# A four-layer hybrid kernel on one core: the last mamba chunk's gating and normalisation moved, one drive given to ScalarE, the mixtures' last lists moved ahead

## The reference

```python
x = x + mamba(_layernorm(x))       # 256 channels, 16 states each, a scan over 2048 tokens
x = x + ffn(_layernorm(x))         # mixture of 8 experts
x = x + attention(_layernorm(x))   # linear attention, head size 64
x = x + ffn(_layernorm(x))         # the same mixture again

def _layernorm(x, eps=1e-05):
    return (x - mean(x)) / sqrt(var(x) + eps)
# mamba: x_m, z = split(x @ W_in); x_m = silu(conv(x_m) + conv_b); dt = softplus(...)
#   state = exp(dt * A) * state + dt * B * x_m ;  y = sum_s(state * C) + x_m * D
#   out = (y * silu(z)) @ W_out
# ffn: scores = (tanh(x @ gate_w.T) + 1) / 2; each expert takes its 512 best tokens (top_k);
#   layernorm, two layers with gelu, times the score, added at the tokens' rows (at[idx].add)
```

## Time and profile before

| what | us |
|---|---|
| time, median of 3 runs | 832.78 (832.06 to 836.05) |
| the profiled execution | 831.78 |
| its span | 830.0 |

### The profile page before, as it was taken

The page is one execution under the profiler, slowest core; times in us unless marked ns, Lnnn a source line. Parts: engine busy times, 40 slices in busy tenths (PEclk is TensorE's granted clock), DMA queues, the critical chain, the costliest instruction groups (busy, mean ns, idle before and its releaser), DMA issues. The chain is left out here.

```text
span 830.0 us, 11428 instructions
## 1 busy us (share of the span) xinstructions
PE 621.2 (75%) x3747; PEld 465.3 (56%) x3747; DVE 569.7 (69%) x1030; ACT 504.8 (61%) x1020; POOL 605.9 (73%) x427
## 2 busy tenths in 40 slices
PE   6767999799996999967778824999462871489842
PEld 4334766577674777746667713766342760367531
DVE  6357998989989898999998687423115669832210
ACT  2257999879899779997889366423112359222300
POOL 6019899999999999998899571778861026378875
PEclk8987999989998999989899955899885995589967
DMA  5044765745546475565453065523334004053332
GB/s 155 0 132 134 220 213 179 231 155 203 222 166 199 161 237 185 160 216 182 183 189 132 1 197 147 156 40 40 40 28 111 1 1 102 21 156 43 39 36 25
DMA packets 71131, 104.52 MB, mean 126 GB/s; under 512 B 15545, under 2 KB 49122, under 8 KB 71074
## 3 DMA queue, kind: packets, MB, share of 16 engines
q1 hardware_dynamic: 59122, 93.58, 35.3%
q0 software_dynamic: 11264, 8.66, 7.8%
q10 hardware_dynamic: 688, 1.57, 0.7%
HBM read 90.12 MB, written 13.63 MB: 125 GB/s over the span
## 5 line engine op out<-in xcount | busy, mean ns | idle before, releaser
L412 POOL TENSOR_TENSOR product<-state,c_all 128x1024 f32<-128x1024 f32 x128 | 301.9, 2401 | 19.8 <-DVE state L730 16.2
L934 PE MATMUL m_psum<-ident,product 128*128 128x128 f32 x1024 | 137.8, 280 | 10.0 <-POOL product L412 5.0
L934 PEld LDWEIGHTS m_psum<-ident,product 128*128 128x128 f32 x1024 | 118.5, 145 | 31.5 <-issue 14.3
L730 DVE TENSOR_TENSOR_SCAN state<-decay,carry,m_psum 128x1024 f32<-128x1024 f32 x56 | 129.5, 2336 | 5.3 <-issue 2.7
L545 ACT ACTIVATE decay<-dt,decay_rate 128x1024 f32<-128x1024 f32 x112 | 126.8, 1143 | 10.2 <-DVE state L730 8.3
L730 DVE TENSOR_TENSOR_SCAN state<-decay,m_psum 128x1024 f32<-128x1024 f32 x56 | 125.9, 2276 | 8.8 <-PE m_psum L958 3.4
L523 ACT ACTIVATE drive_T<-dtu_T,b_T 128x128 f32<-128x128 f32 x416 | 130.0, 394 | 0.9 <-PE m_psum L958 0.7
L1453 ACT ACTIVATE f_f_T<-f_psum,f_b_T 128x512 f32<-128x512 f32 x64 | 44.0, 688 | 136.2 <-PE f_psum L1712 136.2
L1394 POOL DMA_INDIRECT f_got<-f_table,f_tokens x64 | 65.4, 1021 | 56.8 <-DVE f_tokens L1563 41.0
L836 PE MATMUL m_psum<-xn_T,w_tap 128*128 128x512 f32 (+2 forms) x128 | 71.6, 673 | 21.6 <-DVE dt L677 16.0
L958 PE MATMUL m_psum<-ident,drive_T 128*128 128x128 f32 x544 | 74.0, 280 | 9.9 <-DVE state L730 9.6
(11 more groups left out here) (266 smaller groups left out, 1086.9 us busy)
## 6 DMA issues: line engine op xcount, KB each, us to landing
c_all<-cb_dram SPq DMA_DIRECT2D x128, 512.0 KB, 4.1
b_all<-cb_dram SPq DMA_DIRECT2D x16, 512.0 KB, 4.9
f_table<-f_rows SPq DMA_DIRECT2D x2, 2176.0 KB, 12.2
X<-in_L_attn_a_x SPq DMA_DIRECT2D x4, 512.0 KB, 7.3
f_w_raw<-in_L_ffn_fc2s SPq DMA_DIRECT2D x1, 2048.0 KB, 17.6
between<-f_f SPq DMA_DIRECT2D x1, 2048.0 KB, 9.2
X<-between SPq DMA_DIRECT2D x4, 512.0 KB, 6.1
out<-f_f SPq DMA_DIRECT2D x1, 2048.0 KB, 9.3
```

Source lines behind the costliest of these rows:

```text
L412: pool.tensor_tensor(product[:, n % RING, :], state[:, n % RING, :], c_all[:, n % RING, :], ALU.mult).then_inc(product_ready, 1)
L730: dve.tensor_tensor_scan(state[:, n % RING, :], flat(pair(n)) if alone else decay[:, n % RING, :], lone_drive[:, made(n, "lone") % LONES, ...
L934: last = pe.matmul(psum[:, Y + i // BT, i % BT * P:(i % BT + 1) * P], product[:, n % RING, i * P:(i + 1) * P], ident[:], start=(s == 0 and ...
```

## The change

1. Epsilon goes into the bias of ScalarE's square root (a new tile `eps`, filled by POOL at the start). VectorE's separate add of epsilon goes, in all layer norms: four times in the mamba layer (L628), four in each front (L1069) and once more where a front normalises its result a second time (L1094), twice in attention (L1817).
2. In the last chunk, drive 6 changes from 'd' to 'a'.
3. In the last chunk, z's matmuls stand at TensorE's steps 15 to 18 (before 15, 18, 19, 22). Roots and Silus stand together at ScalarE's step 21 (before: roots at 15, Silus at 25). VectorE's two scale operations stand at step 22 (before 16 and 17). ScalarE normalises at steps 25 to 30 (before 20 to 27), and TensorE turns those tiles at 27, 28, 29 and 31 (before 25 to 28).
4. In the mixtures lists(3) stands earlier on TensorE, ahead of `turn_rows(0)`, and in mixture 1 ahead of six weight turns too; VectorE takes them ahead of `scale_rows(0, 0)`. The first weight turn stands at search step 6 instead of 5 (`LATE`).

```diff
-        MEASURE_AT, AGGREGATE_AT, ROOT_AT, SCALE_AT, NORMALISE_AT = FRONT + 1, FRONT + 9, FRONT + 15, FRONT + 16, FRONT + 20
+        MEASURE_AT, AGGREGATE_AT, SCALE_AT, NORMALISE_AT = FRONT + 1, FRONT + 9, FRONT + 22, FRONT + 25
+        LAST_SILU, BY_STEP = FRONT + 21, (0, 3, 6, 9, 12, 14, 16)
...
-        MAKERS = ('dddqqadpadaaadad', 'qdaaqaddaapppdaa')
+        MAKERS = ('dddqqadpadaaadad', 'qdaaqaddaapppdaa') * 3 + ('dddqqaapadaaadad', 'qdaaqaddaapppdaa')
...
-        F_AT = (25, 26, 27, 28)
+        F_AT, LAST_Z_AT = (27, 28, 29, 31), (15, 16, 17, 18)
...
-                if n == ROOT_AT:
+                if n == LAST_SILU:
                     act.preload_act_table(ACT.Sqrt)
                     for q in range(2):
                         front["root"](act, q)
-                    act.preload_act_table_set("natural_log_exp_and_others")
...
-                if n % PERIOD == SILU:
+                if (n == LAST_SILU) if g + 1 == CHUNKS else (n % PERIOD == SILU):
                     silu(g)
...
-                    if n == SCALE_AT + q:
+                    if n == SCALE_AT:
                         front["scale"](dve, q)
...
-        dve.wait_ge(aggregated, QT * (q + 1))
-        dve.tensor_scalar(rstd[:, part(q)], moments[:, part(q), 1], LN_EPS, None,
-                          ALU.add).then_inc(variance, 1)
 
     def root(act, q):
-        act.wait_ge(variance, q + 1)
-        act.activation(rstd[:, part(q)], rstd[:, part(q)],
-                       ACT.Sqrt).then_inc(std_done, 1)
+        act.wait_ge(aggregated, QT * (q + 1))
+        act.activation(rstd[:, part(q)], moments[:, part(q), 1], ACT.Sqrt,
+                       bias=eps[:]).then_inc(std_done, 1)
...
-    SCORES, LATE, MIDWAY = 4, 5, 6
+    SCORES, LATE, MIDWAY = 4, 6, 6
...
+        take_lists(3)
         scale_rows(0, 0)
-        take_lists(3)
...
-            for n in range(MIDWAY, 2 * E):
+            for n in range(MIDWAY, MIDWAY + 4):
+                turn_weights(n)
+        lists(3)
+        if first_use:
+            for n in range(MIDWAY + 4, 2 * E):
                 turn_weights(n)
...
         turn_rows(0)
-        lists(3)
```

More of the change, by code:

```diff
@@ L33, in layer_norm_constants, with mamba @@
     return at + 2 * tiles
-def mamba(nc, X, ident, w_tap, early, front, home, gate_w, x, W_in, conv_w, conv_b, A_log, D, W_x, W_dt, b_dt, W_out):
+def mamba(nc, X, ident, eps, w_tap, early, front, home, gate_w, x, W_in, conv_w, conv_b, A_log, D, W_x, W_dt, b_dt, W_out):
     BATCH, L, DM = x.shape
@@ L221, in beside @@
             out += [("turn", g, 1, t, (TURN_AT[1],)) for t in range(TB)]
-            out += [("z", g, i // TB, i % TB, (Z_AT[i],)) for i in range(KB * TB)]
+            out += [("z", g, i // TB, i % TB, ((Z_AT if g + 1 < CHUNKS else LAST_Z_AT)[i],)) for i in range(KB * TB)]
             out += [("back", g, 0, t, (BACK_AT[0],)) for t in range(TB)]
@@ L452, in std @@
             def std(first, end):
-                act.wait_ge(variance, end)
-                part = rstd[:, first * CT:end * CT]
-                act.activation(part, part, ACT.Sqrt).then_inc(std_done, 1)
+                act.wait_ge(dve_chain, 2 * CT * end + (1 if first else 0))
+                part = slice(first * CT, end * CT)
+                act.activation(rstd[:, part], moments[:, part, 1], ACT.Sqrt, bias=eps[:]).then_inc(std_done, 1)
             def take_turned(g):
@@ L592, in _ @@
                         front["root"](act, q)
-                    act.preload_act_table_set("natural_log_exp_and_others")
-                if n >= NORMALISE_AT and 2 * (n - NORMALISE_AT) < 2 * QUARTER:
+                if NORMALISE_AT <= n < NORMALISE_AT + len(BY_STEP) - 1:
                     if n == NORMALISE_AT:
                         act.wait_ge(summed, FRONT)
-                    front["normalise"](act, "a", 2 * (n - NORMALISE_AT), 2 * (n - NORMALISE_AT) + 2)
-                if n % PERIOD == SILU:
+                    front["normalise"](act, "a", *BY_STEP[n - NORMALISE_AT:n - NORMALISE_AT + 2])
+                if (n == LAST_SILU) if g + 1 == CHUNKS else (n % PERIOD == SILU):
                     silu(g)
@@ L606, in _ @@
                         drive_by_act(n + ahead, first, first + CT // 2)
+            for number, piece in enumerate(PIECES):
+                if piece[0] in ACT_LATER and piece[4] and piece[4][-1] + ACT_LATER[piece[0]] >= STEPS:
+                    take(piece, number)
             act.preload_act_table(ACT.Sqrt)
@@ L627, in token_stats @@
                                           lambda i: X[:, g * CT + i, :], CT)
-                dve.tensor_scalar(rstd[:, tiles], moments[:, tiles, 1], LN_EPS, None,
-                                  ALU.add).then_inc(variance, 1)
                 return at
@@ L1010, in _ @@
         def _(pool):
+            pool.memset(eps[:], LN_EPS)
             pool.memset(ident[:], 0.0).then_inc(zeroed, 1)
@@ L1024, in front_tiles, with front_of @@
             for what, shape in shapes.items()}
-def front_of(nc, tiles, name, X, home, banks, scores, gate_pad, makers, takers):
+def front_of(nc, tiles, name, X, home, eps, banks, scores, gate_pad, makers, takers):
     def sem(what):
@@ L1091, in variance_again @@
         dve.tensor_tensor(again[:], again[:], moments[:, :, 1],
-                          ALU.mult).then_inc(link, 1)
-        dve.wait_ge(link, 2)
-        dve.tensor_scalar(again[:], again[:], LN_EPS, None, ALU.add).then_inc(variance2, 1)
+                          ALU.mult).then_inc(variance2, 1)
     def root_again(act):
         act.wait_ge(variance2, 1)
-        act.activation(again[:], again[:], ACT.Sqrt).then_inc(std2_done, 1)
+        act.activation(again[:], again[:], ACT.Sqrt, bias=eps[:]).then_inc(std2_done, 1)
     def scale_again(dve):
@@ L1721, in mixture, with attention @@
     return sync, gpsimd, scalar, vector, tensor, load
-def attention(nc, ctx, X, ident, room, front, x_loaded, wq, wk, wv, wo):
+def attention(nc, ctx, X, ident, eps, room, front, x_loaded, wq, wk, wv, wo):
     HD, DM = wq.shape
@@ L1815, in vector @@
             at += TB
-            dve.wait_ge(chain, at)
-            dve.tensor_scalar(rstd[:, part], moments[:, part, 1], LN_EPS, None,
-                              ALU.add).then_inc(variance, 1)
             dve.wait_ge(std_done, h + 1)
@@ L1874, in root @@
             part = slice(h * TB, (h + 1) * TB)
-            act.wait_ge(variance, h + 1)
-            act.activation(rstd[:, part], rstd[:, part], ACT.Sqrt).then_inc(std_done, 1)
+            act.wait_ge(chain, 2 * TB * (h + 1))
+            act.activation(rstd[:, part], moments[:, part, 1], ACT.Sqrt, bias=eps[:]).then_inc(std_done, 1)
         def normalise(first, end):
@@ L2027, in build @@
             home_2 = {"f_at": lambda i: room["f"][:, i, :], "f_T": room["f_T"], "psum": room["psum"]}
-            front_2 = front_of(nc, front_tiles(nc, rest, "f2", TILES, T // J), "f2", X, home_2,
+            front_2 = front_of(nc, front_tiles(nc, rest, "f2", TILES, T // J), "f2", X, home_2, eps,
                                (4, 5, 7, 6, 4, 5, 7, 6), 3, early["gate_pad"], "apaapaap" * 3 + "apdapdad",
@@ L2031, in build @@
             first = mixture(nc, X, ident, room, front_1, "f1", between, True, reloaded, **experts)
-            middle = attention(nc, rest, X, ident, room, front_2, reloaded, **linear)
+            middle = attention(nc, rest, X, ident, eps, room, front_2, reloaded, **linear)
             second = mixture(nc, X, ident, room, front_2, "f2", out.rearrange("b l d -> (b l) d"), False, (),
```

19 lines of the change are left out of this document (8 added, 11 removed).

## The result

| | before | changed |
|---|---|---|
| median of 20 executions, us | 832.09 | 838.41 |
| lowest and highest | 830.25 to 836.59 | 833.14 to 841.77 |
| profiled execution, us | 831.78 | 834.25 |
| its span | 830.0 | 832.5 |

The ratio is 1.0049, with a 95% interval of 1.003 to 1.0068: slower by 4.1 us, by half a per cent. The forecast was 836.6 (+3.8), with a range of 829.5 to 841.0. The medians are 6.3 apart and the profiled spans only 2.5. Of the changed kernel's 20 executions seven lie between 833 and 835 and eleven between 838 and 842: its median falls into the upper group, and the profiled execution belongs to the lower one.

What follows compares the result with a forecast made beforehand. VectorE bounds the last chunk (busy 101.47 of 107.00 us), the first scatter's start the mixtures. Terms -1.8 + 3.5 - 0.2 + 0.8 - 0.8 + 2.3 = +3.8 gave a median of 836.6 us, range 829.5 to 841.0.

Steps and rivals of the forecast that it cites:

- the two waits on ScalarE: Last chunk: late exponents on ScalarE make scans 4 and 20 wait, losing 3.15 and 5.39 us.
- one held scale operation: Last chunk, step 22: POOL's product holds one of VectorE's two scale operations, 2.1 us; none or two also possible.
- Start: Start to first convolution matmul: without the epsilon adds the copies end sooner, -1.8 us (-1.3 to -2.2).
- Last chunk: Last chunk of front 1: gains of 7.8 us against losses by scans 4, 20 and scale operations, net +3.5.
- scan 4: Last chunk: its exponent stands behind drive 8, which waits for drive 5's slot; 3.15 us lost.
- Scan 20: Last chunk: table loads, roots and Silus of ScalarE's step 21 stand ahead of its exponent; 5.39 us lost.
- Rest of front 1: End of front 1: the LayerNorm loses one add of 0.17 us with its hand-over, -0.2.
- Mixture 1: Before mixture 1's first scatter: lists(3) moved ahead exposes the scaling of the first rows, +0.8 us (0.7 to 1.0).
- Attention and front 2: Attention and front 2: four exposed adds of 0.17 us and their hand-overs go, -0.8 (-0.6 to -1.0).
- Mixture 2: Before mixture 2's first scatter: later first layer costs 1.4 us after slack, up to 3.2 with slow clock; +2.3 taken.
- the dearer case: Mixture 2's first layer: clock stays at 0.50 over all eight matmuls, 1.8 us more, 3.2 in all.
- The *rival* on the other side: Last chunk: ScalarE is not late for the lone steps 4 and 20; sum -4.7, 828.1 us; chance 0.15.

Runs made afterwards that it cites:

- the kernels with idle matmuls: Idle matmuls added in TensorE's waits of the start, to the changed kernel and to the kernel before: medians 835.98 and 832.96 us.
- the kernels of the last section: Kernel before with epsilon, z sooner, Silus at 22; then idle matmuls, scale operations apart, drive 6 by ScalarE added in turn: ratios 0.9888, 0.9852, 0.9866, 0.9854.

## Why the prediction was right, and where it was off

The prediction's sign, its place and its size held: the last chunk, where the change was to help, became 3.5 us longer, by the two waits on ScalarE and one held scale operation that it named. That the total came so near is in part luck: the six stages with a forecast moved by +3.6 together, against +3.8, but three of them were off by 1.0 each, one up and two down, and the stages forecast at 0 moved by -1.1.

- *Start*: the first convolution matmul came 1.74 sooner (forecast 1.8). "The chain behind that matmul is serial, so it keeps this" was true of the order and not of the time: with the same code the chain took from 40.6 to 45.7 us by TensorE's clock, a range wider than the gain, against 42.87 before. The step lacked this. Of the 6.3 between the medians up to 3 may belong to it (6.3 less the 3.0 between the kernels with idle matmuls); that is not shown.
- *Last chunk*: measured from the start of one scan to that of the next, drive 6 gave 1.31 (forecast 1.30), each add 2.00 (1.89 and 1.86), z 2.53 (2.42); scan 4 came 3.81 later (3.15, the rest for TensorE's sums), and the scale operations at step 22 cost 2.58 (0.62 and 2.1). Two terms were mis-sized, and they cancel. The departure of the scale operations from steps 16 and 17 shortened these steps by 1.37, not 0.30, for one of them had been held there too (0.92 at 417.10). Scan 20 came 6.65 later, not 5.39: 1.05 of that departure lies between scan 17, with whose end ScalarE's step 21 starts, and scan 20, so VectorE only came sooner and waited for ScalarE. ScalarE's own way there was as forecast (11.40 against 11.22; the roots with their bias took 0.49, not 0.31). That one scale operation was held was a choice between cases in the working, so that this 2.1 fits is luck. The sum hit 3.52 against 3.5 with errors of both signs.
- *Rest of front 1*: -0.2 forecast, +0.46 measured. The forecast named POOL's last product and gave it nothing; it ends 3.27 us behind the start of this stretch (462.98), where it was 2.73 (461.60). POOL's last rows of products, first before, then after the change:

```profile
454.61 6.99 POOL L412 TENSOR_TENSOR product<-state,c_all 128x1024 f32<-128x1024 f32 x3 [0.46 <-DVE state L730]
```

```profile
446.71 16.27 POOL L412 TENSOR_TENSOR product<-state,c_all 128x1024 f32<-128x1024 f32 x7
```

POOL used to wait for VectorE's scans here; now it makes seven products without a break and TensorE's last sums wait for it. The kernel with epsilon alone, which keeps the wait for z, keeps POOL's wait (0.48); this fits a part of z's gain being paid here, though no run of its own shows it. With the changed kernel's order this stretch took 19.8 us in four runs and 21.2 to 21.3 in the others, and TensorE's clock goes with that: over its last 5 us the granted clock was 1.00 in the four and 0.66 to 0.68 in the others.
- *Mixture 1*: a mis-sized term. 0.8 was forecast; undoing the part gave back 1.4 to the first scatter and 1.1 behind it. The scaling was exposed, for 1.00 of TensorE's wait. For the rest the rows show two things together: ScalarE's copies, which alternate with the weight turns, stood still for 4.17 us beside lists(3) and had to start again behind it, and the first sixteen turns there took 3.50 us to the start of the next (531.34 to 534.84), at a granted clock of 0.57 from 531.3 to 534.6, where sixteen took 2.67 at 1.00 with the lists as before. So TensorE's total was not "as it was"; which of the two weighs more is not shown. Why the end behind the first scatter came later too is argued from POOL's longer wait (4.00 against 2.46), not shown by a run of its own.
- *Attention and front 2*: -0.8 forecast, -1.77 measured; the changed code took 56.1 to 59.4 in eleven kernels, the old one 57.9 and 60.4, so the row doesn't settle its size. Again the clock goes with it: 59.4 to 60.4 at a granted clock of 0.75, 56.1 to 57.9 at 0.79 to 0.83.
- *Mixture 2*: 1.4 was the forecast without the clock, 2.3 the value taken; 1.30 and 1.41 were measured. The clock rose within the first layer in spite of the wait of 3.07 us ahead of it: 5.20 us for the eight matmuls, against 5.38 before. The Trainium skill, TensorE: Matmul & The Clock Gate, § Part 1: The HAM clock gate, says that the default is the slow level and that activity lifts it. This trace agrees that the layer began slow (a granted clock of 0.50 from 735.8 to 737.4), but it began slow before the change too (0.50 from 730.8 to 732.5), so nothing was lost. The kernel with Silus at step 22 took 24.7 instead of 23.5 us between the last one-hot rows and the first scatter, with a first layer of 6.31 us at 0.58, so the dearer case exists.
- The *rival* on the other side (scans 4 and 20 not late) was false, and both waits could be removed by order alone; that is what makes the kernels of the last section faster. The Trainium skill, SBUF — State Buffer, § Who interferes with whom, says that a VectorE operation with two inputs in SBUF and a POOL instruction that reads SBUF contend, and that whichever comes first keeps the other out. The trace agrees for the scale operations: the one that began while POOL's product ran ended with it (434.60 against 434.58), and the one that began with it was not held (0.17).

## What to carry to other kernels

Work taken off the busiest engine is only worth what the engine that feeds it can follow with: look in the other engine's program order at what now stands ahead of the one instruction that the busy engine needs next, and at which of these wait for something (here a slot, three table loads). A tiny operation that costs 2 us beside a long instruction of another engine is worth removing before anything larger is moved. And when a kernel's executions fall into groups, compare stages of traces, and put the groups' cause under control before reading a half per cent from medians.

## What the runs showed of the hardware that was not expected

A serial stretch of TensorE work with waits of 1 to 2 us took from 40.6 to 45.7 us with the same instructions: groups at 3.67 or 5.37 us, with a granted clock of 0.79 or 0.51 from 44 to 52 us in the two shown. Some 30 idle matmuls in these waits held the clock there at 1.00 and the stretch at 40.2 to 41.7 us in five kernels. The spread of whole executions came down from 6 to 9 us to 2 to 3 in three of the five, and was 5.6 and 8.0 in the other two. The first convolution group stayed slow even so (5.37 and 6.73 us for eight matmuls in two of these kernels).

Later stages have the same pattern: the first layer of mixture 1 took 3.6 us at a granted clock of 1.00 and 5.25 to 6.37 at 0.57 to 0.69, the rest of front 1 and attention differed by 1.4 and by 1.5 to 4 us with the clock. Before a term of about 1 us is read from two traces, the granted clock of that stage has to be the same in both.
